# Twenty-four half-megabyte sign pieces through eight half buffers in a three-layer decoder kernel

## What is computed

```python
x = layernorm(x + attn(x))                # causal self-attention, 16 heads of 32
x = layernorm(x + softmax_attn(ctx) @ x)  # x @ attention of the context with itself
x = layernorm(x + ffn(x))                 # ternary weights
# x: (4, 512, 512), ctx: (4, 512, 256), all float32; hidden width 2048
def ffn(x):
    xq = activation_quant(rms_norm(x))            # 8-bit rows
    g = silu(xq @ sign(W_g).T)
    p = g * (xq @ sign(W_u).T)
    return p @ sign(W_d).T
```

## Time and profile before

| what | us |
|---|---|
| median of 3 runs | 622.56 |
| the runs | 625.86, 622.56, 620.17 |
| profiled execution, its time | 619.0 |
| its span, first to last instruction | 617.3 |

### The profile page before, as it was taken

One profiled execution on the slowest core, in us unless ns is written; L12 is line 12 of the kernel. 1 busy time (PEld: TensorE's weight loads), 2 busy tenths in 40 slices (PEclk: granted clock), 3 DMA queues, 4 the chain that ended last, 5 costly groups with the idle time before them and its releaser, 6 DMA issues.

```text
span 617.3 us, 13871 instructions
## 1 busy us (share of the span) xinstructions
PE 583.5 (95%) x5100; PEld 389.1 (63%) x5100; DVE 487.6 (79%) x1296; ACT 413.0 (67%) x773; POOL 395.0 (64%) x518
## 2 busy tenths in 40 slices
...
GB/s 302 323 206 230 253 174 53 129 256 86 10 47 105 91 70 37 49 158 91 78 39 46 146 69 19 3 103 120 36 51 53 105 87 36 10 90 56 19 35 34
DMA packets 90851, 60.29 MB, mean 98 GB/s; under 512 B 65056, under 2 KB 81952, under 8 KB 89248
## 3 DMA queue, kind: packets, MB, share of 16 engines
...
q10 hardware_dynamic: 544, 0.52, 0.3%
...
## 4 chain that ended last, share of the span: by engine, by line
PE 66%; SPq 11%; DMA 6%; DVE 6%; ACT 6%; issue 3%; POOL 2%; ACTq 0%; POOLq 0%; DVEq 0%
PE ps_b L700 24%; PE ps_b L851 16%; PE ps_b L866 14%; SPq L635 9%; PE ps_b L795 4%; PE ps_b L774 4%; PE ps_b L757 2%; DMA st<-qk 2%; PE ps_b L753 1%; DMA oT<-ohl 1%; DMA bx<-in_b_x_dram 1%; DVE ps_b L1122 1%; ACT ps_b L961 1%; ACT p L947 1%; ACT ph L884 1%
## 5 line engine op out<-in xcount | busy, mean ns | idle before, releaser
L1122 DVE CUSTOM_DVE_ANT_0 ps_b<-ps_b,future 128x256 f32<-128x256 f32 (+3 forms) x256 | 118.7, 517 | 16.9 <-PE ps_b L757 10.4
L1317 POOL TENSOR_TENSOR ph<-p,ph 128x512 f16<-128x512 f32 x96 | 110.0, 1161 | 27.2 <-ACT ph L884 26.5
L851 PE MATMUL ps_b<-xqT,sg 128*128 128x256 f16 x1024 | 124.9, 272 | 0.1
L866 PE MATMUL ps_b<-sd,hp 128*128 128x512 fp8e4 x512 | 119.1, 379 | 0.0
L1313 POOL TENSOR_TENSOR hp<-gt,hp 128x512 f16<-128x512 f32 x64 | 74.0, 1161 | 56.6 <-ACT hp L884 56.2
L851 PEld LDWEIGHTS ps_b<-xqT,sg 128*128 128x128 fp8e4 x1024 | 98.0, 98 | 19.0 <-ACT p L947 0.6
L700 PE MATMUL ps_b<-xhl,wh 128*128 128x256 f16 x480 | 84.8, 275 | 1.4 <-DVE wl L1073 1.3
L866 PEld LDWEIGHTS ps_b<-sd,hp 128*128 128x128 f16 x512 | 48.6, 98 | 50.0 <-POOL hp L1313 1.5
L1274 POOL TENSOR_SCALAR_AFFINE_SELECT p<-p 128x256 f32<-128x256 f32 (+1 forms) x96 | 46.5, 494 | 46.2 <-ACT p L947 45.7
L700 PE MATMUL ps_b<-xhl,wl 128*128 128x256 f16 x240 | 66.0, 275 | 0.0
L947 ACT ACTIVATE p<-ps_b 128x512 f32<-128x512 f32 x96 | 54.1, 594 | 16.8 <-PE ps_b L774 16.5
...
## 6 DMA issues: line engine op xcount, KB each, us to landing
...
```

Of the source, the lines that this page charges most:

```text
L851: ins = pe.matmul(ps[:, a * HALF:(a + 1) * HALF], sg[:, ("gg", "uu").index(name), c, ht * P:(ht + 1) * P], xqT[:, c, :], start=c == 0, sto ...
L866: ins = pe.matmul(ps[:, :], hp[:, (UNITS * s + n) % HP_SLOTS, h, a, t * P:(t + 1) * P], sd[:, ht, :], start=ht == h == 0, stop=ht == HT - ...
L1122: ins = dve.tensor_tensor_reduce(scores, scores, future[:, S - width:S], 1.0, -3e38, ALU.add, ALU.max, tops[:, g // 2, j:j + 1, g % 2, qt ...
L1317: pool.tensor_tensor(out_, in_, hi, ALU.subtract).then_inc(signal, 1)
```

## The change

The twelve pieces are cut in two along the free dimension, to 24 pieces of 512 KB, and each of the four regions is cut into two half buffers, numbered 0 to 7. `SIGN_PLACE` says which piece goes where: pieces 0 to 7 in the eight buffers, 8 to 13 and 14 to 19 in 0, 1, 2, 3, 6 and 7, and 20 to 23 in 0 to 3. A load waits for the sign that last used its buffer; the first load of a buffer waits for the low halves of the attention weights which stood in that region. Each buffer has a semaphore of its own.

Three waits are new or other: the loads of the rows (lr0, lr1) wait for 20 signs, and no longer for `w_lo` 13; ov on ScalarE (steps 0 and 1) waits for six signs; gg and uu wait for 24.

All five orders are new. On ScalarE sg0 to sg18 now stand before the first exponential st0.0.0.0, and sg19 to sg23 among st and hi of step 0.0. Before, sg0 to sg4 stood ahead of st0.0.0.0, sg5 to sg7 in the attention of steps 0.0 and 0.1, and sg8 to sg11 after the word tx0.0.1. Also ahead of st0.0.0.0 now: qk0.1.3, va0.1.1, ta0.2, en0.3 and ez0.3. Ahead of qk0.0.0, which stood before ws2.3 and ws3, now stand ws2.3, ws3, cs0.0 and cs0.1. On SyncE bi stands before lw2.2, lg0 to lg7 before the first sk, and lg8 to lg23 among sk0.0 and sk0.1, the words ta0.0 to ta0.2, sh0.0.0 and sh0.0.1. On GpSimd the four rb of steps 0.0 and 0.1 stand behind the last st of step 0.0, no longer ahead of its first. From step 1.0 on the lists hold the same words, in an order that differs in places.

```diff
+SIGN_PLACE = (*range(8), *2 * (0, 1, 2, 3, 6, 7), *range(4))
+SIGN_PIECES = len(SIGN_PLACE)
...
+def last_sign(where, i=SIGN_PIECES):
+
+    return max((n + 1 for n in range(i) if SIGN_PLACE[n] in where), default=0)
...
+        def sign_stage(k):
+            return stage[k // 2][:, k % 2 * S * 2:(k % 2 + 1) * S * 2]
...
             def load_signs(i):
-                if i < 2:
-                    sp.wait_ge(w_lo, 4 * (i + 1))
+                k = SIGN_PLACE[i]
+                if last_sign((k,), i):
+                    wait_for(sp, signs, last_sign((k,), i))
                 else:
-                    sp.wait_ge(signs, i - 1)
-                sp.dma_start(stage[i % 2], sgT[i]).then_inc(weight_in[i % 2], 16)
+                    wait_for(sp, w_lo, min(4 * (k // 2 + 1), 13))
+                sp.dma_start(sign_stage(k), sgT[i // 2][:, i % 2 * S * 2:(i % 2 + 1) * S * 2]).then_inc(sign_in[k], 16)
...
             def load_rows(s):
                 b, h = divmod(s, 2)
                 if s < 2:
-                    sp.wait_ge(w_lo, 13)
+                    wait_for(sp, signs, last_sign((6, 7)))
...
             def gate_or_up(name, s, n):
-                wait_for(pe, signs, 12)
+                wait_for(pe, signs, SIGN_PIECES)
...
             def sign_piece(i):
-                act.wait_ge(weight_in[i % 2], 16 * (i // 2 + 1))
-                if i < 8:
-                    dst = sg[:, i // 4, i % 4, :]
+                k, (piece, half) = SIGN_PLACE[i], divmod(i, 2)
+                act.wait_ge(sign_in[k], 16 * SIGN_PLACE[:i + 1].count(k))
+                if piece < 8:
+                    dst = sg[:, piece // 4, piece % 4, half * S * 2:(half + 1) * S * 2]
                 else:
-                    dst = sd[:, 4 * (i - 8):4 * (i - 7), :].rearrange("p h n -> p (h n)")
-                act.activation(dst, stage[i % 2], ACT.Sign, saturate=False).then_inc(signs, 1)
+                    first = 4 * (piece - 8) + 2 * half
+                    dst = sd[:, first:first + 2, :].rearrange("p h n -> p (h n)")
+                act.activation(dst, sign_stage(k), ACT.Sign, saturate=False).then_inc(signs, 1)
...
             def low_products(s, g):
                 wait(act, pv_done, s, HG * (g + 1))
                 if s >= 2:
                     wait(act, to_lo, s - 1, 0)
+                else:
+                    wait_for(act, signs, last_sign((4, 5)))
```

More of the change, by code:

```diff
@@ L100 @@
 SP_ORDER = """
[L101 to L105, removed]
@@ new lines @@
+lg7 sk0.0.0.3 lg8 sk0.0.0.0 lg9 sk0.0.0.1 lg10 sk0.0.0.2 lg11 lg12 sk0.0.1.3 lg13 lg14 sk0.0.1.0 lg15 sk0.0.1.1 lg16
+lx2 lg17 sk0.0.1.2 lg18 lg19 ta0.0 lg20 sh0.0.0 sk0.1.0.0 lg22 sk0.1.0.2 sk0.1.0.3 sk0.1.0.1 lg23 ta0.1 lg21 ta0.2
+sh0.0.1 sk0.1.1.3 lr1 sk0.1.1.0 lx3 lr0 sk0.1.1.1 sk0.1.1.2 sh0.1.0 sh0.1.1 to0.0.0 to0.0.1 lc1 ta0.3 sk1.0.0.1
+sk1.0.0.0 sk1.0.0.3 sk1.0.0.2 tx0.0.0 tx0.0.1 sk1.0.1.2 sk1.0.1.1 sk1.0.1.0 sk1.0.1.3 to0.1.0 to0.1.1 lx4 sh1.0.0
+tq0.0.0 tq0.0.1 tx0.1.0 tx0.1.1 sk1.1.0.3 sk1.1.0.2 sk1.1.0.0 sk1.1.0.1 sh1.0.1 ta1.0 sk1.1.1.3 sk1.1.1.1 sk1.1.1.2
@@ L119 @@
[L119 to L123, removed]
@@ L129 @@
[L129 to L133, removed]
@@ L196 @@
 """
 ACT_ORDER = """
-lx0 xs0.0.0 ws0.0 xs0.0.1 ws0.1 ws0.2 ws0.3 ws1.0 ws1.1 bv ws1.2 ws1.3 ws2.0 ws2.1 ws2.2 wx qk0.0.0 ws2.3 ws3 cs0.0
-qk0.0.1 cs0.1 sg0 qk0.0.2 qk0.0.3 va0.0.0 sg1 cp0.0 cp0.1 va0.0.1 xs0.1.0 xs0.1.1 en0.0 qk0.1.0 sg2 qk0.1.1 ez0.0
-en0.1 nm0.0.0 ta0.0 ez0.1 sg3 en0.2 qk0.1.2 va0.1.0 ez0.2 ta0.1 sg4 st0.0.0.0 qk0.1.3 hi0.0.0.0 st0.0.0.1 va0.1.1
-nm0.0.1 st0.0.0.2 st0.0.1.0 st0.0.1.1 hi0.0.0.1 hi0.0.0.2 hi0.0.1.0 xs1.0.0 xs1.0.1 sg5 ov0.0.0 st0.0.1.2 hi0.0.1.1
-sg6 hi0.0.1.2 ta0.2 qk1.0.0 st0.0.2.0 st0.0.2.1 nm0.1.0 st0.0.2.2 ov0.0.1 hi0.0.2.0 hi0.0.2.1 hi0.0.2.2 st0.0.3.0
@@ L204 @@
-st0.0.3.1 qk1.0.1 st0.0.3.2 hi0.0.3.0 hi0.0.3.1 sx0.1.0.2 sg7 hi0.0.3.2 ov0.0.2 st0.1.0.0 st0.1.0.1 st0.1.0.4
-hi0.1.0.0 sx0.1.0.3 ov0.0.3 st0.1.1.0 hi0.1.0.1 hi0.1.0.4 st0.1.1.1 to0.0.0 hi0.1.1.0 sx0.1.0.5 sx0.1.0.6 sx0.1.1.2
-nm0.1.1 to0.0.1 st0.1.1.4 sx0.1.1.3 sx0.1.1.5 sx0.1.1.6 qk1.0.2 st0.1.2.0 st0.1.2.1 ov0.1.0 sx0.1.2.2 hi0.1.1.1
-hi0.1.1.4 en0.3 hi0.1.2.0 ez0.3 st0.1.2.4 st0.1.3.0 qk1.0.3 st0.1.3.1 ov0.1.1 hi0.1.2.1 hi0.1.2.4 sx0.1.2.3 st0.1.3.4
-sx0.1.2.5 sx0.1.2.6 sx0.1.3.2 tx0.0.0 ta0.3 hi0.1.3.0 hi0.1.3.1 sx0.1.3.3 sx0.1.3.5 sx0.1.3.6 hi0.1.3.4 ov0.1.2
@@ L244 @@
[L244 to L247 removed]
+lx0 xs0.0.0 xs0.0.1 ws0.0 ws0.1 ws0.2 ws0.3 ws1.0 ws1.1 ws1.2 ws1.3 ws2.0 ws2.1 ws2.2 ws2.3 ws3 wx bv cs0.0 cs0.1
```

425 lines of the change are left out of this document (223 added, 202 removed).

## The result

The changed kernel is slower: 627.65 us median (625.22 to 630.5, 20 runs) against 621.48 (618.63 to 628.23, 20 runs), ratio 1.0094, 95% interval 1.0075 to 1.0114. The forecast was 619; the time lies inside the range of 610 to 630, on the other side of no change. The profiled execution took 630.5 us (span 628.8), the longest of its 20 runs, and that of before was one of the shorter ones. So the two spans lie 11.5 us apart where the medians lie 6.2, and only the places of the differences are taken from the profile.

The account below looks back on a forecast made before the run. ScalarE's attention stage of steps 0.0 and 0.1 was taken to set TensorE's full supply, near 110 us. Work to 109.6 plus 6.5 of waits gave 116.1 against 119.4, so 622.6 less 3.3 made 619 us; range 610 to 630.

Parts of the forecast that it names:

- Price and sum of ScalarE's work: ScalarE up to tx0.0.1: 0.95 us a half piece; start 19.8, then 35.5 and 54.3 us of work, 109.6 without waits.
- What waits are left: ScalarE's waits up to tx0.0.1: 2.5 us ahead of the first exponential, 4 us within the stage, together 6.5.
- SyncE's queue: SyncE's issues in steps 0.0 and 0.1: twelve more, 6.3 us, but the first stack load some 4 us sooner; nothing net.
- the two cancel: On SyncE, added load issues against an earlier start: step 0.0's last stack load at about 45 us before and after.
- three marks named for a wrong forecast: sh0.0.0 landing after 58 us; signs waiting over 2 us for loads; TensorE's idle behind 142 us over 2 off 10.8.
- The premise that ScalarE's stage sets the point: Attention of steps 0.0 and 0.1 on ScalarE sets TensorE's full supply near 110 us; tx0.0.1 and the end 3.3 us sooner.
- The 20.00 of 20 us: ScalarE's busy time between 90 and 110 us in the kernel before, taken as evidence that its stage sets the point.
- The queue in front of the scores: Rival, 0.20: on SyncE, maxima, transposes and stack loads stand behind half loads; first exponential at 63 to 64 us, end some 629.
- Hidden anyway: Rival, 0.11: ScalarE's stage waits for scores and GpSimd, so saved sign work becomes longer waits; nothing moves, 622.6 us.
- rb on GpSimd at nothing: Four rb, 5.0 us, now among masks and low halves on GpSimd: counted as nothing; without cover a mask delayed by 3.8.
- Smaller loads: Half pieces in a full DMA queue cost only their bytes, at 364 GB/s; nothing added to the sum.
- The lists from step 1.0 on ... no change, with 2 us to either side: Later lists, with 10.8 us of TensorE's idle time left there: no change, 2 us to either side.

Follow-up runs that it names:

- new_half_old_rest: Changed kernel's lists up to the attention of step 1.1 (some 290 us), then those of the kernel before; 627.44 us, ratio 1.01 to the kernel before.
- the run with the gap: Changed kernel, last seven signs and loads late, old lists behind 290 us, three rb moved into GpSimd's gap at 78 to 81.6 us; 623.85 us, ratio 1.0056.

## Why the prediction was wrong

It forecast 3.3 us to be won and 6.2 were lost. ScalarE's work was counted rightly; the waits and the premise were wrong. That 627.65 us lies inside the range of 610 to 630 is owed to the rivals' share in it, not to the sum.

- *Price and sum of ScalarE's work: right.* A half sign lasts 1.04 to 1.07 us (1.05 said). 35.78 us of work from the first projection to the first exponential stand against 35.5; in the stage it was 51.7 against 54.3, less than forecast. The first projection came at 20.51 us, not 19.8: inside its bounds, and nothing was gained there.
- *The step that failed is "What waits are left".* It took 2.5 and 4 us; the rows show 5.9 (41.69 less 35.78) and 8.9 (59.77 less 50.91). The 2.5 us were for sh0.0.0, held in SyncE's list by sg14 and by loads. sg14 was done at 48.4 us; what held the row was the issue of ta0.0, now in front of it, with 4.98 us that had no term in the sum, and then a landing of some 5.5 us. Of the 5.9 us only 1.5 are the wait for the scores behind that row; sign loads (1.7), matmuls (1.3), a stack load (0.8) and smaller waits are the rest. Within the stage some 4.9 us are waits for scores (6.3 less 1.45), 1.8 for a transpose and 1.8 for maxima on their way through TensorE. The sum put no price on what the bytes do to small transfers: with 3.7 MB in the calm of before, stack loads and rows of maxima land late (the transposes don't: 6.2 us in the middle, where two took 8.5 and 9.2). The earlier trace rows had the size of it, a stack load at 6.1 us behind two pieces; about that became usual (median 5.8), and the prediction used it for a rival only.
- *SyncE's queue: "the two cancel" was wrong.* The issues of step 0.0's stack loads end at 48.3 us (45.94 and 2.34), not at 45. Loads were counted by their issue, 0.52 us, and not by what they do to the landing of what follows.
- *sh0.0.0 landed after 58 us* (TensorE starts on it at 61.57), one of the three marks named for a wrong forecast. TensorE's idle time behind 142 us, 14.3 for 10.8, is another. The third, signs that wait more than 2 us for loads, didn't come: it was 1.7 us in all.
- *The premise that ScalarE's stage sets the point, and the end with it, did not hold.* Taking some 5.6 us of signs (seven times 1.05 less 0.25) out of ScalarE's list changed nothing; and with tx0.0.1 2.0 us sooner than before the kernel was still some 3 us slower. But ScalarE's list isn't far behind the rows: with the rows on another queue, and with the loads shortened, it came to the first exponential without a wait, at 62.38 and 60.86 us. Two limits lie within 1.5 us of each other there, so taking away one of them shows little of what it costs. The 20.00 of 20 us didn't tell which of them sets the point.
- *The rivals.* "The queue in front of the scores" is what happened: it was to decide from a first exponential later than 59.9 us (it was 62.20) and gave some 629. Its mechanism was half right: moving a row of maxima, to an earlier place or to another queue, won nothing; moving the last loads and their signs out of the way, or cutting the loads' bytes, did. That its 629 comes so close is partly luck, as 3.8 us of it are for rb, which no run shows. "Hidden anyway" also holds as far as signs go: shorter signs became longer waits.
- *rb on GpSimd at nothing* is open: the run with the gap puts another delay in its place. *Smaller loads: right in the main*: 353 GB/s with halves queued, and 2 us for the pieces alone. The Trainium skill ("DMA: Bandwidth & Descriptors", section Bandwidth) names about 358 GB/s for each core when both cores of an HBM domain stream. The mean of 353 is near that, but from 20 to 30 us this trace shows 398, so 358 was no limit here.
- *"The lists from step 1.0 on ... no change, with 2 us to either side"* was on the low side, inside its bounds as far as is known: 3.3 us of idle time near 350 us, some 1.6 us by the marks from first to last gate matmul, and between nothing (new_half_old_rest) and 1.4 us (1.0027 after 1.005) in the ratios. What the lists from 150 to 290 us cost wasn't told apart.

In ratios: 2.7 to 2.8 us for the last seven loads (1.0094 less 1.005 or 1.0049), about 2 for the halves in lists as they were, 0 to 1.6 for the later lists. Together that is close to the 6 us, but each is uncertain by about 2 us. That the halves' 2 us are the same in the new lists wasn't tried, and neither was a kernel with both the seven signs and the seven loads shortened in place. So the bytes of the last seven loads are shown to cost nearly half of the loss; for the rest the account is a sum of such parts. What the DMA engines do among themselves isn't seen.
